# Laying out five of eight head groups by DMA through DRAM instead of by selection matmuls, in an attention and expert kernel on one Trainium2 core

## What is computed

```python
def reference(x, cond, ...):
    x = x + attn(modulate(x, cond), w_qkv, w_out)       # 16 heads of 8, rotary, causal softmax
    x = x + ffn(experts(x, cond))                       # 2 shared + top 2 of 8 routed; then top 3 of 8 zones
# attention, per batch
q, k = rope(q), rope(k)                                 # after qkv = x @ w_qkv.T
scores = einsum('bhsd,bhtd->bhst', q, k) / sqrt(8)      # causal
out = softmax(scores) @ v @ w_out.T
```

## Time and profile before

| | us |
|---|---|
| median of 3 runs | 205.31 (204.97 to 205.75) |
| the profiled execution | 205.4 |
| its span in the trace | 203.7 |

### The profile page before, as it was taken

One profiled execution on the slowest core, in us unless ns is written; L12 is line 12 of the kernel. 1 busy time (PEld: TensorE's weight loads), 2 busy tenths in 40 slices (PEclk: granted clock), 3 DMA queues, 4 the chain that ended last, 5 costly groups with the idle time before them and its releaser, 6 DMA issues.

```text
span 203.7 us, 3373 instructions
## 1 busy us (share of the span) xinstructions
PE 187.9 (92%) x1034; PEld 131.2 (64%) x1034; DVE 141.5 (69%) x459; ACT 147.7 (73%) x245; POOL 85.1 (42%) x100
## 2 busy tenths in 40 slices
PE   7994999999999997998999999999799989999993
PEld 3753766666666663664466776776557857788881
DVE  4584689888888885898027798468979845566552
ACT  4487848677878776879774485465688899899980
POOL 4616068461336363743332261021356962198000
PEclk9999799999999999999999999999999999999999
DMA  5602321229633233332111199600000000001001
GB/s 155 219 0 52 101 67 41 53 52 316 215 91 88 70 102 91 83 103 72 34 52 45 37 326 340 169 0 0 0 3 2 0 0 0 2 3 52 0 0 52
DMA packets 9509, 15.72 MB, mean 77 GB/s; under 512 B 2116, under 2 KB 3268, under 8 KB 9364
## 3 DMA queue, kind: packets, MB, share of 16 engines
q1 hardware_dynamic: 8916, 15.12, 24.5%
q10 hardware_dynamic: 576, 0.39, 0.6%
HBM read 9.16 MB, written 2.42 MB: 57 GB/s over the span
## 4 chain that ended last, share of the span: by engine, by line
PE 68%; DVE 15%; ACT 11%; issue 4%; POOL 1%; DVEq 0%; ACTq 0%; POOLq 0%
PE psum L1271 10%; PE psum L1400 9%; PE psum L1322 8%; PE psum L1402 8%; PE psum L1401 8%; PE psum L1302 6%; DVE psum L617 3%; PE psum L1305 2%; PE psum L1194 2%; PE psum L1254 2%; PE psum L1139 2%; DVE t_raw L763 2%; PE psum L1306 1%; ACT t_q_pad L991 1%; PE psum L1255 1%
## 5 line engine op out<-in xcount | busy, mean ns | idle before, releaser
L617 DVE CUSTOM_DVE_ANT_0 psum<-psum,t_causal 128x128 f32<-128x128 f32 (+3 forms) x128 | 59.5, 523 | 15.5 <-PE psum L1271 14.9
L939 ACT ACTIVATE t_probs<-psum 128x768 f32<-128x768 f32 (+1 forms) x48 | 41.3, 883 | 4.0 <-PE psum L1302 3.0
L1271 PE MATMUL psum<-t_stacked,t_q_pad 128*128 128x256 f32 (+2 forms) x128 | 36.9, 361 | 0.6 <-ACT t_q_pad L886 0.2
L515 POOL TENSOR_SCALAR_AFFINE_SELECT t_probs<-t_probs 128x512 f32<-128x512 f32 x32 | 20.0, 638 | 32.4 <-ACT t_probs L939 32.4
L1271 PEld LDWEIGHTS psum<-t_stacked,t_q_pad 128*128 128x128 f32 x128 | 22.0, 190 | 13.8 <-DVE t_row_max L617 9.8
L781 DVE SCALAR_TENSOR_TENSOR t_q_pad<-psum,t_zw_all,t_q_pad 128x512 fp32r<-128x512 f32 x24 | 17.9, 749 | 11.6 <-ACT t_q_pad L989 11.6
L975 ACT ACTIVATE t_raw<-psum 128x512 f32<-128x512 f32 x24 | 14.3, 595 | 10.4 <-PE psum L1446 7.7
L1322 PE MATMUL psum<-t_probs,t_v_all 128*32 128x512 f32 (+3 forms) x256 | 20.5, 439 | 0.0
L549 POOL TENSOR_TENSOR t_q_pad<-t_raw,t_q_pad 128x512 fp32r<-128x512 f32 x8 | 10.3, 1290 | 20.1 <-ACT t_q_pad L991 20.1
L1302 PE MATMUL psum<-t_q_mov,t_k_pad 128*128 128x512 f32 (+1 forms) x64 | 18.3, 371 | 0.2
L617 DVE DVE_READ_ACCUMULATOR2_ANT t_row_max<- 128x1 f32 x128 | 18.2, 142 | 0.0
(11 more groups left out here) (236 smaller groups left out, 420.9 us busy)
## 6 DMA issues: line engine op xcount, KB each, us to landing
t_k_pad<-t_stacked SPq DMA_DIRECT2D x32, 64.0 KB, 2.0
t_probs<-in_L_ffn_Wa SPq DMA_DIRECT2D x2, 1024.0 KB, 8.7
t_q_pad<-t_stacked SPq DMA_DIRECT2D x28, 64.0 KB, 2.0
scratch<-t_o_sb SPq DMA_DIRECT2D x7, 256.0 KB, 2.0
t_raw<-in_experts SPq DMA_DIRECT2D x1, 1792.0 KB, 7.6
t_raw<-in_rotary SPq DMA_DIRECT2D x2, 256.0 KB, 4.9
out_dram<-t_probs SPq DMA_DIRECT2D x2, 256.0 KB, 2.0
t_raw<-in_w_all ACTq DMA_DIRECT2D x2, 128.0 KB, 3.0
```

The costliest lines, as they stand in the source:

```text
L515: last = G.affine_select(out=tri, in_=tri, compare_op=ALU.is_ge, fill=0.0, base=0, pattern=[[0, HG], [1, P]], channel_multiplier=-1)
L617: last = V.tensor_tensor_reduce(scores, scores, causal[:, S - width:S], 1.0, 3 * BIG, ALU.add, ALU.max, row_max[s][:, qb, j:j + 1])
L939: A.activation(probs[s][:, c, 2 * h2:2 * h2 + 2, 0:w], ST[:, slot_of("exp", n, u):slot_of("exp", n, u) + 2, 0:w], ACT.Exp, scale=float(1.0 ...
L1271: last = T.matmul(ring("max", n, u)[:, i * 2 * P:i * 2 * P + width], q_pad[s][:, j, qb * P:(qb + 1) * P], stacked[:, 2 * n + 1, 0:width], ...
```

## The change

Groups 3 to 7 are no longer stacked by PE. SP writes the high and low rows to `scratch` in their stacked order (`spill`; six DMAs for group 3 from batch 0's parts, six for groups 4 to 7 from batch 1's) and the block of zeros and ones from a new DRAM array `rest` (`spill_rest`, DRAM to DRAM). `load_stacked` reads q and k of a group back, 256 KB each, and the pads of these groups read DRAM too. SP waits for the landed spills before the first load of each batch. The last selection matrix, the stacking matmuls of these groups and their ACT copies are gone. The parts' buffers are free again when the spills have landed. The weights come in seven loads of 256 KB in passes 1 to 4, are split one group later (chunks 0 to 6 in passes 3 to 6), and the reciprocal and product move to units 80 and 93.

```diff
-STACK_IN = {0: 3, 1: 4, 2: 5, 3: 6, 4: 7}
+BY_PE = 3
-INV_AT = [78, 88]
-SPLITS = {(2, 0): 0, (2, 2): 1, (3, 0): 2, (3, 2): 3, (4, 0): 4, (4, 2): 5, (5, 0): 6}
+INV_AT = [80, 93]
+SPLITS = {(3, 0): 0, (3, 2): 1, (4, 0): 2, (4, 2): 3, (5, 0): 4, (5, 2): 5, (6, 0): 6}
+EXPERT_LOADS = [(), (0, 1), (2, 3), (4, 5), (6,), (), (), ()]
...
             def pad_q(n):
...
-                sp.wait_ge(rep_copied, 3 if n == 1 else 2 * n + 3)
+                if n < BY_PE:
+                    sp.wait_ge(rep_copied, 3 if n == 1 else 2 * n + 3)
...
-                    sp.dma_start(f32_of(q_pad[s][q, j, :]), f32_of(stacked[q, 2 * n, :])).then_inc(q_padded[s], 16)
+                    src = f32_of(stacked[q, 2 * n, :]) if n < BY_PE else laid(n, 0)[q, :]
+                    sp.dma_start(f32_of(q_pad[s][q, j, :]), src).then_inc(q_padded[s], 16)
...
+            def spill(b, i):
+                q = slice(0, P) if b else slice(32 * BY_PE, P)
+                sp.wait_ge(hi_ready, 4 * b + (i + 1 if b else 3 + i))
+                for r in ((1, 2), (1, 3))[i]:
+                    sp.dma_start(laid_blocks(b, i)[r], f32_of(qk_hi[q, i, :])).then_inc(spilled, 16)
+                sp.wait_ge(lo_ready, 4 * b + (i + 1 if b else 3 + i))
+                sp.dma_start(laid_blocks(b, i)[(3, 2)[i]], f32_of(qk_lo[q, i, :])).then_inc(spilled, 16)
+            def load_stacked(n):
+                for i in (1, 0):
+                    sp.dma_start(f32_of(stacked[:, 2 * n + i, :]), laid(n, i)).then_inc(ld_stack[n], 16)
...
             pad_k(0)
+            spill_rest()
...
             pad_q(1)
+            spill(0, 0)
+            spill(0, 1)
...
+            sp.wait_ge(rest_rows, 16 * 2)
+            sp.wait_ge(spilled, 16 * SPILLS)
             for n in range(GROUPS):
+                if n == 1:
+                    sp.wait_ge(spilled, 2 * 16 * SPILLS)
                 if n + 3 < GROUPS:
+                    load_stacked(n + 3)
                     pad_q(n + 3)
+                if n == 0:
+                    spill(1, 0)
                 if n + 2 < GROUPS:
                     pad_k(n + 2)
+                if n == 0:
+                    spill(1, 1)
                 if n == NG:
                     spread_inverse(0)
                 if n < GROUPS - 1:
                     store_sums(n)
-                if n == 0:
-                    sp.wait_ge(v_ready, B)
-                    sp.wait_ge(roped_ready, 6)
-                    sp.dma_start(raw[:], io["experts"]).then_inc(ld_raw, 16)
+                for k in EXPERT_LOADS[n]:
+                    load_experts(k)
                 if n == NG - 1:
                     gather(0)
...
+                        pe.wait_ge(ld_stack[n], 16 * 2)
...
-                if n in STACK_IN:
-                    stack(2 * STACK_IN[n])
-                    stack(2 * STACK_IN[n] + 1)
```

More of the change, by code:

```diff
@@ L48 @@
 LEAD, FIRST = 8, 3
-STACK_IN = {0: 3, 1: 4, 2: 5, 3: 6, 4: 7}
+BY_PE = 3
+SPILLS = 6
 ST_ORDER = [("stack", 2), ("project", 1)]
 for _n in range(GROUPS):
-    ST_ORDER += [("exp", _n, _u) for _u in range(4)] + ([("stack", STACK_IN[_n])] if _n in STACK_IN else [])
-    ST_ORDER += [("exp", _n, 4), ("exp", _n, 5)]
+    ST_ORDER += [("exp", _n, _u) for _u in range(STU)]
 def max_units(n, i):
@@ L300, in program @@
         k_padded = [sem(f"k_padded{s}") for s in range(2)]
+        ld_stack = {n: sem(f"ld_stack{n}") for n in range(BY_PE, GROUPS)}
         stored = [sem(f"stored{s}") for s in range(2)]
         xc_ready = [sem(f"xc_ready{k}") for k in range(3)]
+        ld_raw = [sem(f"ld_raw{k}") for k in range(len(SPLITS))]
         block = ctx.enter_context(nc.Block())
@@ L346, in hidden_of, with laid, laid_blocks @@
             return pair_of(i)[:, 1, :]
+        def laid(n, i):
+            return scratch[GROUPS + 1 + i * (GROUPS - BY_PE) + n - BY_PE]
+        def laid_blocks(b, i):
+            first = GROUPS + 1 + i * (GROUPS - BY_PE) + (NG - BY_PE if b else 0)
+            slots = scratch[first:first + (NG if b else NG - BY_PE)]
+            return slots.rearrange("g (j r d) t -> r (g j) d t", j=HG, r=KB)
         def slot_of(*item):
@@ L387, in pad_k, with spill_rest @@
                     q = slice(32 * j, 32 * j + 32)
-                    sp.dma_start(f32_of(k_pad[s][q, j, :]), f32_of(stacked[q, 2 * n + 1, :])).then_inc(k_padded[s], 16)
+                    src = f32_of(stacked[q, 2 * n + 1, :]) if n < BY_PE else laid(n, 1)[q, :]
+                    sp.dma_start(f32_of(k_pad[s][q, j, :]), src).then_inc(k_padded[s], 16)
+            def spill(b, i):
[5 more added lines that the diff above has]
+                sp.dma_start(laid_blocks(b, i)[(3, 2)[i]], f32_of(qk_lo[q, i, :])).then_inc(spilled, 16)
+            def spill_rest():
+                for i in range(2):
+                    first = GROUPS + 1 + i * (GROUPS - BY_PE)
+                    slots = scratch[first:first + GROUPS - BY_PE]
+                    rows = slots.rearrange("g (j r d) t -> r (g j) d t", j=HG, r=KB)[0]
+                    sp.dma_start(rows, io["rest"][i].unsqueeze(0).broadcast_to(
+                        [(GROUPS - BY_PE) * HG, HD, S])).then_inc(rest_rows, 16)
+            def load_stacked(n):
+                for i in (1, 0):
+                    sp.dma_start(f32_of(stacked[:, 2 * n + i, :]), laid(n, i)).then_inc(ld_stack[n], 16)
             def store_sums(n):
@@ L472, in _ @@
             G.tensor_tensor(dinv[:], dvar[:], dexp[:], ALU.pow).then_inc(dinv_ready, 1)
-            for g in range(2, NG):
+            for g in range(2, BY_PE):
                 G.memset(f32_of(sel[:, g, :, :]), 0.0).then_inc(sel_zero, 1)
@@ L1611, in laid_out @@
     rot = swapped(wq[:2 * D])
+    rest = np.zeros((2, HD, S), np.float32)
+    rest[1, 0:2] = 1.0
     small = np.zeros((P, W_END), np.float32)
```

70 lines of the change are left out of this document (34 added, 36 removed).

## The result

The changed kernel takes 200.32 us (median of 4 runs, 200.07 to 200.64), the kernel before in the same session 205.39 (204.97 to 205.75): ratio 0.9755, 95% interval [0.9732, 0.9778]. The forecast was 200.0, range 198.3 to 203.0. The span fell from 203.7 to 198.6 us.

A forecast was written before the change was run, and what follows sets the result against it. The prediction took PE to bound windows 1 to 3, with DVE close behind and bounding window 0. Stacking's 5.70 us less 0.16 (window 5) and 0.2 (window 6) gave 5.34 us saved: forecast 200.0 us, range 198.3 to 203.0.

The forecast's parts named there:

- Part 1: Attention windows, one pass each: without stacking, windows 1 to 4 fall to 8.85 us, window 0 gains nothing; 5.70 us saved.
- The hole of window 4: PE stood 1.42 us before L1305 as ACT's split waited for stacking; gone with stacking, window 4 saves 2.71 us.
- Part 2: Reciprocal moves into window 5 (0.14 us less DVE work), product into window 6; later splits charged 0.2 us there.
- Part 3: SP's queue and transfers: issues and bytes fit a window on average; order matters at three places; 0.3 us charged.
- (a): Before window 0: SP's two DRAM copies and six spills, 2.0 to 3.5 us, delay group 2's q pads; cost 0.
- (b): Early window 2: pads behind batch 1's spills land at 51.6 to 53.9, needed at 54.08; room 0.2 to 2.5, cost 0.
- (c): Window 5: group 7's q pads, behind loads and gather, land at 80.3 to 80.7, needed at 80.63; 0.3 us charged.
- 1 (8.70 throughout): Rival: PE alone sets the pace, windows at 8.70 us and window 0 giving 1.0; 198.4 us, chance 0.12.
- 2 (9.24): Rival: DVE sets the pace sooner, a window without stacking is 9.24 us as window 5; 201.5 us, chance 0.13.
- 3: Rival: reads from DRAM land 1.7 us later than pads from SBUF, delaying group 7's pads; 201.9 us, chance 0.12.
- 4, the only slower one: Rival: the DMA queue bounds windows 1 to 4, 10.8 us each at 170 GB/s; 207.8 us, chance 0.07.
- 5: Rival: late group 7 pads and exp or DVE waits take all back; 204.5 to 206 us, chance 0.06.

The follow-up runs named there:

- e1: Kernel before, PE still stacking, with only the weight splits, reciprocal and product moved to the changed kernel's places; 203.63 us, ratio 0.991.
- e5: Changed kernel with four useless 512-column matmuls added on PE in pass 2, where stacking was; 200.94 us, ratio 0.9762.
- e7: Changed kernel with DVE's row maxima over 256 instead of 512 columns in the last four maximum units of groups 1 to 7; 198.26 us, ratio 0.9626.
- e9: Changed kernel with the reordered queue of e3 and maxima leading the exps by 9 units instead of 8; 200.83 us, ratio 0.9745.
- e10: Changed kernel with the reordered queue of e3 and maxima leading the exps by 7 units instead of 8; 198.41 us, ratio 0.9645.
- e4: Changed kernel with four useless 512-column matmuls added on PE in pass 0, where stacking was; 200.19 us, ratio 0.9737.
- e2: Changed kernel with splits, reciprocal and product back at their old places and each expert load one pass earlier; 202.01 us, ratio 0.982.
- e12: Changed kernel run again, unaltered, in another session; 199.95 us, ratio 0.9726.
- e3: Changed kernel with group 7's stacked rows and all expert loads but the last issued ahead of pass 3's store and gather; 199.91 us, ratio 0.9712.
- e8: Changed kernel without the DRAM round trip: groups 3 to 7 reuse stacked rows of groups 0 to 2 in SBUF; 199.84 us, ratio 0.9709.
- e6: Changed kernel with each group's q pads issued before its stacked loads, source still DRAM; 200.70 us, ratio 0.9746.

## Why the prediction was right

**Part 1, stacking (5.70 forecast, 5.26 measured over windows 1 to 4).** The mechanism was right, shown from two sides: taken out of PE the matmuls give 0.68 to 0.96 us a window, put in they cost 0.68 (e1, e5). The mis-sized term is the length of a window without them: 8.85 was an estimate from DVE's idle time in window 5 (8.18 + 0.65), and it is 8.96. The floor of 8.70 was met (8.70 in e7, 8.67 to 8.71 in e9), and that DVE stands between it and the time was right too. But the added 0.26 is not DVE's capacity, of which 10% is free; another lead takes it away (e9, e10), so it hangs on where the wide tiles fall. Four windows by 0.11 are 0.44 us, which is the whole shortfall of the sum (0.38, the other terms being 0.06 better together). It follows that PE's 1.22 us between starts was never worth 1.22: 0.26 of it was lost elsewhere as soon as it was gone.
The hole of window 4 was read rightly from ACT's row: 1.64 of the 2.60 us (e1). By the ratios (0.991 of e1, 0.9755) over a third of the whole gain needs no layout through DRAM at all.
Window 0: nothing, with PE's wait grown from 0.34 to 0.89, as forecast (e4, e7).

**Part 2, moved work.** Window 6 lost 0.13, charged 0.2. Window 5 without a wait is 8.97, where the working has 9.10: the exchange of the product for the reciprocal and the later splits gave 0.24 us in e1, not 0.14. Which of them gave it no run separates. I missed that the product's place is also tied to SP's queue (e2); with the change as written it cost nothing.

**Part 3, SP and the transfers.** (a) and (b) cost nothing: windows 0 to 3 have no length that a DMA set. The room in (b) was small: with two expert loads more ahead, group 4's pads came 0.55 us late (e2). (c) was named as the only place and is, in the profiled run. In e12 it is window 4 instead, where the prediction took a wait for a DMA as a sign of being wrong; that sign did come, at a price of 0.4 us. The 0.3 of (c) measured 0.45 (e3, e8), but the step behind it was wrong: the landing was taken from pads that had nothing large ahead of them, and with the expert loads and the stacked rows ahead it was 3.64 us. Put into the working, that gives 81.9 to 82.3 against a need at 80.63, a cost of 1.3 to 1.7 us. It came out small because the issue was 0.2 to 0.6 us earlier than worked out, and the need 0.4 later (2.12 us into a window, by e3, from 78.91: 81.03), PE's windows being longer than forecast. That the 0.3 was near is luck. So is 9.40 against 9.42, where 9.10 for 8.97 and 0.3 for 0.45 cancelled. The range and the direction do not hang on it: with 1.7 in place of 0.3 the forecast is 201.4.

**The rivals.** 1 (8.70 throughout) failed by the 0.26 us owed to DVE's wide tiles, and in e7 it holds for windows 1 to 3. 2 (9.24) failed: window 5 falls to 9.00 once its product and splits are moved (e1). 3 had the right symptom, landings 1.5 to 1.6 us later, but the price was smaller and the cause another, the bytes ahead in the queue and not DRAM as the source (e6, e8). 4, the only slower one, failed clearly: 226 GB/s with the DMA engines 74% busy, and 264 GB/s with 86% in window 1 of e2, and no window longer than without the traffic (e8). 5 did not come.

## What to carry to other kernels

A layout of operands that a few matmuls do on the busiest engine can go through DRAM at no cost to the engines, if the transfers have slack; what it costs is decided in the order of the issuing queue, and a small transfer just behind large ones should be priced with a landing well above that of one alone (here 3.5 us for 2.0). When an engine is relieved, the next window length is not its own floor: take the floor and add what the ring to the next engine loses at its widest tiles, and try the lead by one unit either way: here one less gave 1.4 us, and one more lost about 0.7. Where an engine stands behind a buffer that is being overwritten, move the overwriter first; here that was over a third of the gain.

## What the runs showed of the hardware

- A 64 KB pad whose source is DRAM held SP's issue 0.42 us (median of 20), one with its source in SBUF 0.59 (median of 8), in the same kernel. So a full window's 8 pads issue in 3.6 us (1.82 + 1.81), not the 4.8 of the prediction.
- A 64 KB pad lands 1.8 to 2.1 us after its issue with nothing large ahead, from DRAM as from SBUF, 2.7 to 3.1 behind 512 KB of stacked rows, and 3.5 to 3.8 behind 1 MB (medians of four; e6, e8, after).
- Single issues took far longer than the median: 1.41 us for a pad, 1.46 for an expert load (medians 0.42 and 0.43). Such an outlier and a late landing together made the wait in e12; the place of the wait is not the same from run to run.
- 187 to 226 GB/s of DMA beside a PE that is busy throughout and a DVE busy 90% lengthened no window by over 0.02 us against e8, nor did 264 GB/s in e2 (8.97).
